# An attention and routed-FFN layer on one core: the next step's rows prepared beside the projection, the planned order made anew, and the tail's rows turned by VectorE

## What is computed

```python
x = inputs @ W_qkv + b_qkv                 # [4,1024,768]
x = x.reshape(B, 16, S, -1)                # 16 heads of S=1024 rows and 16 values each for q, k, v
q, k, v = jnp.split(x, 3, axis=-1)
attn = softmax(q @ k.T * scale + causal_mask)
out = (attn @ v).reshape(B, S, -1) @ W_out + b_out
# ffn: a light FFN (256->128->256) on all rows; a router (50 iterations of coordinate descent)
# picks 256 rows of each batch, and these go through a heavy FFN (256->1024->256) as well
return light_out + heavy_out
```

## Time and profile before

| | us |
|---|---|
| median of 3 runs | 711.55 (711.24 to 713.2) |
| the profiled execution | 714.09 |
| its span, first to last instruction | 712.4 |
| PE busy | 667.8 (94%) |
| DVE busy | 554.8 (78%) |
| ACT busy | 403.5 (57%) |
| POOL busy | 380.6 (53%) |

### The profile page before, as it was taken

One profiled execution on the slowest core, in us unless ns is written; L12 is line 12 of the kernel. 1 busy time (PEld: TensorE's weight loads), 2 busy tenths in 40 slices (PEclk: granted clock), 3 DMA queues, 4 the chain that ended last, 5 costly groups with the idle time before them and its releaser, 6 DMA issues. The chain is left out here.

```text
span 712.4 us, 12474 instructions
## 1 busy us (share of the span) xinstructions
PE 667.8 (94%) x3987; PEld 296.2 (42%) x3987; DVE 554.8 (78%) x1571; ACT 403.5 (57%) x908; POOL 380.6 (53%) x774
## 2 busy tenths in 40 slices
PE   4997999899999999899989999999999999999995
PEld 2653555333323333233323332333333436568665
DVE  4865888999999999999989999999998575152111
ACT  2332222787777777467768877777767554332320
POOL 4686130488775847857957853554442454413303
PEclk9999999999999999979999999999999999999998
DMA  8888996678949649696987944844833323442512
GB/s 276 207 219 196 242 264 179 154 141 129 180 70 161 129 63 163 103 132 111 152 160 99 164 73 52 120 75 51 174 63 29 121 60 92 147 148 88 119 59 30
DMA packets 247057, 92.49 MB, mean 130 GB/s; under 512 B 212992, under 2 KB 232608, under 8 KB 243872
## 3 DMA queue, kind: packets, MB, share of 16 engines
q1 hardware_dynamic: 245456, 89.60, 63.0%
q0 software_dynamic: 1536, 2.10, 1.8%
HBM read 56.65 MB, written 35.01 MB: 129 GB/s over the span
## 5 line engine op out<-in xcount | busy, mean ns | idle before, releaser
L1288 DVE CUSTOM_DVE_ANT_0 ps<-ps,maskrow 128x640 f32<-128x640 f32 (+7 forms) x512 | 375.3, 779 | 30.9 <-PE ps L1039 29.4
L897 ACT ACTIVATE strips<-ps 128x512 f32<-128x512 f32 (+1 forms) x608 | 313.2, 576 | 112.0 <-PE ps L1081 89.5
L1039 PE MATMUL ps<-QTk,QTq 96*128 96x512 bf16 (+3 forms) x768 | 189.2, 335 | 18.5 <-DVE mx L1288 10.6
L1081 PE MATMUL ps<-QTq,QTk 99*128 99x512 bf16 (+3 forms) x768 | 185.4, 331 | 2.8 <-DMA QTq<-m_d 1.9
L1099 PE MATMUL ps<-strips,vext 128*32 128x512 f32 (+3 forms) x1536 | 162.8, 500 | 0.9 <-DVE oT L1311 0.4
L1039 PEld LDWEIGHTS ps<-QTk,QTq 96*128 96x128 bf16 x768 | 53.3, 98 | 166.6 <-DVE mx L1288 133.1
L1081 PEld LDWEIGHTS ps<-QTq,QTk 99*128 99x128 bf16 x768 | 68.2, 98 | 89.3 <-ACT strips L897 41.2
L1739 POOL TENSOR_SCALAR_AFFINE_SELECT strips<-strips 128x512 f32<-128x512 f32 x128 | 79.3, 636 | 43.2 <-ACT strips L897 42.8
L999 PE MATMUL ps<-shared,xrT 128*128 128x384 f32 (+1 forms) x256 | 94.8, 503 | 0.2
L1288 DVE DVE_READ_ACCUMULATOR2_ANT mx<- 128x1 f32 x512 | 72.1, 141 | 0.0
L999 PEld LDWEIGHTS ps<-shared,xrT 128*128 128x128 f32 x256 | 47.3, 196 | 26.8 <-issue 3.1
(11 more groups left out here) (153 smaller groups left out, 689.8 us busy)
## 6 DMA issues: line engine op xcount, KB each, us to landing
pieces_d<-pieces SPq DMA_DIRECT2D x64, 192.0 KB, 3.4
qk<-qkv_d SPq DMA_DIRECT2D x64, 128.0 KB, 4.0
qkv_d<-shared SPq DMA_DIRECT2D x16, 384.0 KB, 3.8
QTq<-pieces_d SPq DMA_DIRECT2D x16, 384.0 KB, 5.2
QTk<-pieces_d SPq DMA_DIRECT2D x16, 384.0 KB, 7.7
vext<-qkv_d SPq DMA_DIRECT2D x16, 256.0 KB, 5.8
QTq<-pieces_d SPq DMA_DIRECT2D x16, 256.0 KB, 5.6
QTk<-pieces_d SPq DMA_DIRECT2D x16, 256.0 KB, 8.3
```

What stands on the lines that cost most here:

```text
L897: nc.scalar.activation(dst, src, ACT.Exp, scale=SCALE).then_inc(exp_done, 1)
L1039: mm = pe.matmul(psM[:, s, at:at + n], QTq[0:W, f % 3, c * 1024 + qb * P:c * 1024 + (qb + 1) * P], QTk[0:W, f % 3, c * 1024 + k0:c * 1024 ...
L1081: mm = pe.matmul(psE[:, (NE * q + j) % ES, k * n:(k + 1) * n], QTk[0:W + 3, q % 3, c * 1024 + kb * P:c * 1024 + (kb + 1) * P], QTq[0:W + 3 ...
L1288: ins = nc.vector.tensor_tensor_reduce(scores, scores, maskrow[:, 1024 - n:1024], 1.0, MASKED, ALU.add, ALU.max, mx[:, f % 2, 8 * c + qb:8 ...
```

## The change

- **Front.** Step 3 is prepared in the front as well (`EARLY` 4): one more turn on DVE (beside tile 23), first piece, split on POOL (ahead of `maxima(0)`) and store. The tables are new: step 1's rows are turned beside tile 12 instead of 10, step 2's beside 16 instead of 15. On SP, step 1's `load_qk` moves from tile 5 to tile 9, behind both parts of step 0's `load_pieces`, which now follow each other at tile 8; the loads of v move from tiles 4 and 13 to 26 and 28; the light weights from 20 to 15.
- **Order.** Four constants of the planner and the estimates of two loads are changed, so the order of the middle is made anew.
- **Tail.** The PE transposes, their ACT copies and `saT`'s two small buffers go. `load_sa` becomes four DMAs in runs of 256 bytes, which put 32x32 blocks in place so that two DVE transposes of 128x512 (`turned`) give the whole unit's turned rows; W_out's rows are loaded in the matching order. PE's output banks become four. ACT computes the light FFN's hidden rows (`hidden`) in new places. `turned(0, 0)` and `turned(0, 1)` stand on DVE ahead of the last step's last `outputs`. The heavy rows' bias is scaled ahead, so one DVE instruction instead of two follows each last product.

```diff
-EARLY, BEGUN = 3, 12
+EARLY, BEGUN = 4, 12
-STEP, PACE = 29.60, 29.94
-SOON, LATER, BEHIND = 0.15, 8.0, 1.44
+STEP, PACE = 28.27, 30.88
+SOON, LATER, BEHIND = 0.15, 9.7, 3.58
-        ("Sync", "LOAD"): [("LOAD", f, part) for f in range(EARLY, STEPS) for part in range(2)],
+        ("Sync", "LOAD"): [("LOAD", f, part) for f in range(3, STEPS) for part in range(2)],
-        return 12.88 * PACE
+        return 12.40 * PACE
-    T_AT = {5: 0, 10: 1, 15: 2}
+    T_AT = {5: 0, 12: 1, 16: 2, 23: 3}
-        psC = ps[:, 4:6]
+        psC = [ps[:, b] for b in (0, 1, 4, 5)]
-                if t in (2, 5, 11, 16):
-                    load_qk((2, 5, 11, 16).index(t))
-                elif t in (4, 13):
-                    load_v(t // 10)
-                elif t == 20:
+                if t in (2, 9, 13, 19, 24):
+                    load_qk((2, 9, 13, 19, 24).index(t))
+                elif t in (26, 28):
+                    load_v((26, 28).index(t))
+                elif t == 15:
                     load_light()
-                elif t in (6, 15, 22):
-                    store_pieces((6, 15, 22).index(t))
-                elif t in (8, 17, 23):
-                    load_pieces((8, 17, 23).index(t), 0)
-                elif t in (9, 18, 24):
-                    load_pieces((9, 18, 24).index(t), 1)
+                elif t in (6, 16, 21, 27):
+                    store_pieces((6, 16, 21, 27).index(t))
+                elif t == 8:
+                    load_pieces(0, 0)
+                    load_pieces(0, 1)
...
             def load_sa(i, u):
-                sp.dma_start(sa_in[:, u], sb3[bass.ds(2 * i + u, 1)].rearrange("a p t e -> (a p) t e")).then_inc(c_in[u], 16)
+                for a in range(4):
+                    sp.dma_start(sa_in[32 * a:32 * a + 32, u].rearrange("p t e -> p (t e)").rearrange("p (m f) -> p m f", m=16),
+                                 sa_blocks[2 * i + u, a]).then_inc(c_in[u], 16)
...
+            def turned(i, u):
+                dve.wait_ge(c_in[u], 16 * 4 * (i + 1))
+                if i > 0:
+                    dve.wait_ge(o_ps, 8 * (i - 1) + 4 * u + 4)
+                elif u > 0:
+                    dve.wait_ge(qk_ps, NE * NQ)
+                blocks = sa_in[:, u].rearrange("p t e -> p (t e)").rearrange("p (m k f) -> p k m f", k=KE, f=32)
+                for k in range(KE):
+                    nc.vector.transpose(saT[u][:, k, :].rearrange("p (m s) -> p m s", s=32), blocks[:, k]).then_inc(saT_done, 1)
+            last_outputs = ("OT", NQ - 1, 1)
             for item in order["Vector"]:
+                if item == last_outputs:
+                    turned(0, 0)
+                    turned(0, 1)
...
+            split(3)
             maxima(0)
```

More of the change, by code:

```diff
@@ L147, in schedule @@
         done["landed", ("LV", f)] = 0.0
-    for f in range(EARLY):
+    for f in range(3):
         done["landed", ("LOAD", f, 1)] = 0.0
+    done["landed", ("STORE", 3)] = 2.0
     def after(*keys):
@@ L615, in layer_kernel @@
         ho_ps = sem("ho_ps")
-        hv_half = sem("hv_half")
+        hb_done = sem("hb_done")
         hv_done = sem("hv_done")
@@ L926, in hidden @@
                 nc.scalar.activation(hT[:, u, :], xrT[:, 0, 512 * (2 * i + u):512 * (2 * i + u) + 512], ACT.Gelu, bias=b1l[:, 0:1]).then_inc(h_done, 1)
[L928 to L937, removed]
             def gathered(h):
@@ L953, in _ @@
             hidden(0, 0)
-            unit(0, 0)
-            unit(0, 1)
+            hidden(0, 1)
             gathered(0)
+            hidden(1, 0)
             heavy_hidden(0, range(4))
-            unit(1, 0)
+            hidden(1, 1)
             heavy_hidden(0, range(4, NHC))
-            unit(1, 1)
+            hidden(2, 0)
             act.wait_ge(gu_done, 2 * NSLOT + 1)
             nc.scalar.activation(gscore[:, :], gu[:, :], ACT.Exp, scale=1.0 / EPS_ROUTE).then_inc(gs_done, 1)
-            unit(2, 0)
-            unit(2, 1)
+            hidden(2, 1)
             gathered(1)
+            hidden(3, 0)
             heavy_hidden(1, range(4))
-            unit(3, 0)
+            hidden(3, 1)
             heavy_hidden(1, range(4, NHC))
-            unit(3, 1, more=False)
         @block.tensor
@@ L1122, in _, with project_c @@
                     ring_item(item)
-            def transposes_c(i, u, t):
+            def project_c(i, u, t):
                 n = 8 * i + 4 * u + t
+                o = psC[n % 4][:, 0:E]
                 if t == 0:
[L1128 to L1132, removed]
+                    pe.wait_ge(h_done, 2 * i + u + 1)
+                if n == 0:
                     for x in slots[-MS:]:
@@ L1135, in transposes_c, with unit @@
                         pe.wait_ge(free[s], at + 1)
-                for k in range(KE):
[L1137 to L1156, removed]
+                    pe.wait_ge(wd_in, 16 * N_WD)
+                elif n == 2:
+                    pe.wait_ge(exp_done, NE * NQ)
+                if n >= 4:
+                    pe.wait_ge(ob_done, n - 3)
+                pe.matmul(o, hT[:, u, t * P:(t + 1) * P], w2l, start=True, stop=False)
+                if t == 0:
+                    pe.wait_ge(saT_done, KE * (2 * i + u + 1))
+                for k in range(KE):
+                    mm = pe.matmul(o, saT[u][:, k, t * P:(t + 1) * P], wout[:, k, :], start=False, stop=(k == KE - 1))
                 mm.then_inc(o_ps, 1)
-            def unit(i, u, more=True):
+            def unit(i, u):
                 for t in range(4):
[L1161 to L1164, removed]
                     project_c(i, u, t)
@@ L1218, in _ @@
             heavy_hidden(1, range(4, NHC))
-            unit(3, 1, more=False)
+            unit(3, 1)
             heavy_out(1, range(4))
@@ L1544, in _ @@
             unit(0, 1, range(2, 4))
+            turned(1, 0)
+            turned(1, 1)
             gathered_invert(1)
             unit(1, 0)
+            turned(2, 0)
             gathered_normalise(1)
@@ L1549, in _ @@
             unit(1, 1)
+            turned(2, 1)
             dve.wait_ge(gs_done, 1)
@@ L1554, in _ @@
             dve.wait_ge(gu_done, 2 * NSLOT + 3)
+            heavy_bias(range(4))
             heavy_rows(range(2))
             unit(2, 0)
+            turned(3, 0)
             heavy_rows(range(2, 4))
             unit(2, 1)
+            turned(3, 1)
+            heavy_bias(range(4, NSLOT))
             unit(3, 0)
```

37 lines of the change are left out of this document (22 added, 15 removed).

## The result

Over 18 runs each, the median is 714.28 us (710.54 to 718.59) after and 712.11 us (709.87 to 714.17) before; the ratio is 1.0033, 95% interval 1.0018 to 1.0048. The changed kernel is slower by about a third of a per cent, where the forecast was 698.2 us. Its profiled execution took 714.54 us and has a span of 712.5 (before: 714.09 and 712.4).

The account below looks back on a forecast made before the run. PE was taken to bound the front, the end of the middle and the tail, DVE the middle. Terms -10.0 + 0.3 - 2.2 - 1.4 = -13.3 from the median 711.55 gave 698.2 us; the 8-in-10 range was 689 to 706.

Parts of the forecast that it names:

- The tail: Last stage: 7.0 us of transposes, 2.6 of idling behind `heavy_hidden` and 0.4 at the end go, together -10.0 us.
- The turns: Tail: 16 DVE transposes of 128x512 take between 9.9 and 11.4 us, at no cost while DVE is idle.
- The load: Tail: a unit's rows in 256-byte runs were taken to land in 6 us, hidden; at 16, 4 us late once.
- rival (c): Tail: the loads come late, 4 us at unit (1, 0), and delay DVE's gathered rows too; 702 us, chance 0.07.
- The front: First stage: 0.7 us off the `QTk` wait, 0.7 lost to step 1's load, 0.3 to step 3's turn; +0.3 us.
- the price of step 1's load: Front: the moved load meets a full queue and DVE's turn waits behind it; 0.7 us lost, between 0 and 3.
- The start of the middle: After the front: step 3's turn leaves (-1.2 us) and 1.0 of low clock is won; -2.2, between 0 and -4.
- The middle's order: DVE-bound middle: the new order wins a tenth of DVE's 14.2 us of waits for C products, -1.4 us.
- rival (b): Middle: the new order wins, DVE's waits fall by half, -7 us; 692 us, chance 0.18.
- (d): Middle: the new order starves DVE, so the kernel is slower; 715 us if waits reach 31 us; chance 0.08.
- The end of the middle: After the last C unit: step 15's E waits for its maxima while PE fills with other work; 0 us.
- rival (a): End of the middle: late router, or XC's issues ahead of step 15's reload; 4 us, at most 8; chance 0.17.

Follow-up runs that it names:

- run 1: The kernel before with the new tail only; front, constants and order as before: 701.67 us against 711.84, ratio 0.9857.
- run 3: The changed kernel with step 1's `load_qk` back at tile 5 and nothing else: 707.98 us, ratio to before 0.9929.
- run 4: The changed kernel with step 0's maxima stored and reloaded on SP ahead of step 3's pieces and the loads of v: 709.57 us, ratio to before 0.9965.
- run 5: The changed kernel with the edits of run 3 and run 4 together: 705.31 us, ratio to before 0.9907.
- runs 7: Run 5 with the planner's constants and load estimates of the kernel before: 700.57 us, ratio to before 0.9845.
- Runs 8 to 10: Kernel before with the router's new pace only, 721.65 us; with all new constants but the pace, 723.18 us; run 5 with the old pace, 713.72 us.
- run 6: Run 5 with XC planned only after step 15's maxima are reloaded, the order behind made anew: 701.74 us, ratio to before 0.986.

## Why the prediction was wrong, point by point

- **The tail: right, but for its load.** -9.2 us from the last PV to the last product (-9.9 there and -10.2 in all in run 1), against -10.0. The terms hold: 0.22 us a tile gone, no idle time behind `heavy_hidden`, one DVE instruction at the end; only `hidden`, taken at nothing, costs PE 0.7 us in the kernel after and nothing in run 1. The turns took 16 x 0.69 = 11.0 us of DVE, between the two bounds; one of them stood 4.1 us for its load, and PE waited for none. The load was mis-sized: 7.3 us a unit at the median where 6 was taken. It was hidden all the same, and rival (c) fell: the rows of unit (1, 0) had landed at 614.8, and PE needed them at 624.0. From the 11 bus cycles for 8 of the Trainium skill's "DMA: Bandwidth & Descriptors", "Why small descriptors are slow", the prediction made an estimate of 27% more, 5.2 us. That page of the Trainium skill calls 27% the overhead, which is 3 cycles' share of 11; 11 for 8 is 37% more, an estimated 5.6 us. The trace agrees with neither, at 7.3 us a unit; a single DMA of the four, 128 KB, took 5.0.
- **The front: the step that failed was the price of step 1's load.** I saw that the load would meet the full queue and placed its landing well: 59 to 61 us, and DVE's turn stands at 61.21. I also named DVE's work behind it. But I took PE's next turn from that alone, 62.5 to 64. It stands at 67.52, since the C unit ahead of it waits for `largest`, which queues behind the turn too. In the front all C units share one slot of the ring (in the kernel's text the other slot's banks are `psT`), so the first late `largest` stops PE. The prediction doesn't name the ring there. The term was +0.3 in all, with +4 as its upper bound; it measured +4.7, and run 3 gave it back.
- **The start of the middle: wrong in sign.** I took 2.2 us off for a turn that goes to the front. But the planner prepares step 4 in the place of step 3, and its turn stands where the old one stood. And I had counted step 3's preparation on DVE and POOL and not on SP: its pieces' store, step 4's `load_qk` and the loads of v, which the change puts ahead of step 0's maxima in SP's queue. I wrote that SP sends the maxima "only three tiles later" and took the place in the list for a time. POOL had the maxima in time, so the split of step 3 ahead of them, which I had priced, wasn't it. From the front's end to the first E unit the start measured +4.9 us, where -2.2 was taken, with 0 as the upper bound. The wait was 4.01 us of it; run 4 took it away and gave 4.7 us.
- **The middle's order: small, as taken, but no gain is shown.** DVE's waits without the one of 5.0 are 13.7 us. The C stage from the first E unit on is 418.3 us long against 420.5, but in the kernel after two more C units of step 1, 2.1 us of DVE's work, are through when the late first E unit starts. Without that wait the new order has 419.0 us (run 5), and the old one 418.0 and 419.0 (runs 7 and 1), so the -1.4 can't be told from 0. Neither rival (b) nor (d) came true in the kernel after: that it was slower, which had a chance of 0.05, came from elsewhere than DVE's waits in the middle. Runs 8 to 10 show that (d) was real all the same: with half of these constants its C stage is up to 9 us longer.
- **The end of the middle: taken at 0, measured +2.9.** The cause was named in rival (a), at a chance of 0.17, with two mechanisms to one price of 4 us. Only one of them counts: XC ahead of the reload, with the order built on it, cost 3.6 us (run 6), the late router's KEY nothing that can be told. PE's fill, which I set against it, did fill the 16 us. What it didn't cover stands behind them: PE's wait for the one-hots, ACT's `hidden` rows, and 1.5 us more of PE's own work up to the last PV (44.3 against 42.8; eight L units stand behind the last C unit instead of seven).

The sum by the measured terms is -9.8 + 4.7 + 2.6 + 2.9 = +0.4 us in the traces; the medians have +2.2. The difference is that of the executions profiled: that of before lies 2.0 us above its median of 18 runs, that of after 0.3. The range, which ended at 706, failed because three terms came out above their upper bounds or near them at once: the front +4.7 (bound +4), the start +4.9 (bound 0), of which 2.1 came back in the C stage, and the end of the middle +2.9 (taken at 0, with 4 in rival (a)). The bounds were set one by one, though runs 3, 4 and 6 trace all three to the order of SP's issues.

## What to carry to other kernels

When a DMA issue is moved, write down the queue's whole list with its blocked stretches, and for each issue behind a blocked one the time when its data was ready and the time when its user needs it: three changes in the order of DMAs cost 12.5 us here (714.28 less the 701.74 of run 6), and no engine's busy time showed it. Before a late instruction is called covered, follow the chain to the second consumer through the ring, with the number of slots that it has in that stage. An order that is made anew can put something else in the place that a change frees, so count on a gap only when the new list shows it.

## What the runs showed of the hardware that I had not expected

- Four issues of runs of 128 bytes, 0.66 us each at the median, took 8.30 and 9.85 us on SP behind two part loads of pieces and a store; with the load out of the way (run 3) two plain stores took the same time there (8.69 us). In the first of these stretches, 50.2 to 58.5 us, the 16 DMA engines are busy for 0.98 of the time. So the delay goes with the place in the queue, not with the kind of DMA, and the issue that stands next pays. I call the queue full there; the trace shows the long issues, not the queue's depth.
- Waits of PE at the ring of 0.2 to 1.4 us, one after the other with only C units in between, stand ahead of stretches at a granted clock of 0.5. Single executions have between 10 and 34 us at that level, and with one and the same order of the middle between 13.5 and 27.3.
